# Constant rows of the score stacks: transfers from a row of ones in place of GpSimd memsets

## The reference

```python
x = x + L0_xattn(layernorm(x), ctx, ctx)          # linear attention to the context
x = x + L0_attn(layernorm(x), pos)                # attention over the batch axis
x = x + L0_ffn(layernorm(x))                      # 8 routed experts (top 2) and 2 shared
x = x + L1_xattn(layernorm(x), ctx, mask)         # softmax attention, 16 heads, 4096 keys
x = x + L1_attn(layernorm(x))                     # pre-norm self-attention with RoPE, and an MLP
x = x + L1_ffn(layernorm(x))                      # self-attention, then 8 experts (top 2)
...
scores = jnp.einsum('bhqd,bhkd->bhqk', q, k)
attn = jax.nn.softmax(scores, axis=-1)
out = jnp.einsum('bhqk,bhkd->bhqd', attn, v)
```

## Time and profile before

| | |
|---|---|
| median of 3 timed runs | 2186.85 us |
| the profiled execution, its own time | 2169.82 us |
| its span | 2168.1 us |
| TensorE (PE) busy | 1772.3 us, 82% |
| VectorE (DVE) busy | 1378.9 us, 64% |
| ScalarE (ACT) busy | 1063.2 us, 49% |
| GpSimd (POOL) busy | 464.2 us, 21% |
| granted TensorE clock, mean | 0.899 |

### The profile page before, as it was taken

One profiled execution on the slowest core, in us unless ns is written; L12 is line 12 of the kernel. 1 busy time (PEld: TensorE's weight loads), 2 busy tenths in 40 slices (PEclk: granted clock), 3 DMA queues, 4 the chain that ended last, 5 costly groups with the idle time before them and its releaser, 6 DMA issues.

```text
span 2168.1 us, 35268 instructions
## 1 busy us (share of the span) xinstructions
PE 1772.3 (82%) x14036; PEld 978.8 (45%) x14036; DVE 1378.9 (64%) x2137; ACT 1063.2 (49%) x1834; POOL 464.2 (21%) x347
## 2 busy tenths in 40 slices
PE   7998948888769888945999999999995578757876
PEld 5566635555547777621333333333332244523443
DVE  2231264251076999859999999999917654236456
ACT  3311112666543666410999999999980034112510
POOL 3212132676413666530000000000002000200000
PEclk9998969999978999975999999999997688968968
DMA  7113011777625565337335352433002611063100
GB/s 288 54 63 131 1 39 33 228 233 229 201 69 176 190 200 191 93 53 110 78 64 96 54 106 54 86 75 74 22 2 30 79 16 40 20 83 35 41 0 20
DMA packets 134880, 198.15 MB, mean 91 GB/s; under 512 B 20886, under 2 KB 100136, under 8 KB 130476
## 3 DMA queue, kind: packets, MB, share of 16 engines
q1 hardware_dynamic: 133052, 191.56, 35.2%
q0 software_dynamic: 1664, 4.33, 0.7%
HBM read 144.55 MB, written 50.99 MB: 90 GB/s over the span
## 4 chain that ended last, share of the span: by engine, by line
DVE 39%; PE 39%; SPq 7%; DMA 5%; issue 5%; POOL 3%; ACT 3%; DVEq 0%; ACTq 0%; POOLq 0%
DVE mx_part L2103 24%; SPq L754 4%; PE bank L1143 3%; PE pair L1484 3%; DVE w_lo L1924 3%; PE pair L1176 2%; DVE mx L2193 2%; PE bank L1279 2%; PE bank L999 2%; PE bank L248 2%; PE bank L1388 2%; PE bank L306 2%; DMA xT<-x_slots 1%; PE bank L1043 1%; PE pair L1338 1%
## 5 line engine op out<-in xcount | busy, mean ns | idle before, releaser
L1653 ACT ACTIVATE pexp_all<-bank 128x512 f32<-128x512 f32 x1024 | 551.9, 596 | 94.6 <-PE bank L1293 81.1
L2103 DVE TENSOR_REDUCE mx_part<-pair 128x2 f32<-128x1024 f32 x512 | 582.9, 1213 | 13.3 <-PE pair L1265 11.1
L1279 PE MATMUL bank<-pexp_all,vst 128*17 128x256 f32 x4096 | 321.6, 386 | 6.0 <-issue 6.0
L1265 PE MATMUL pair<-kst,qs 49*128 49x512 f16 x1024 | 210.1, 407 | 41.1 <-DVE mx_part L2103 28.3
L1293 PE MATMUL bank<-qs,kst 52*128 52x256 f16 x2048 | 203.4, 271 | 0.0
L1265 PEld LDWEIGHTS pair<-kst,qs 49*128 49x128 f16 x1024 | 50.4, 93 | 269.6 <-DVE mx_part L2103 215.3
L1293 PEld LDWEIGHTS bank<-qs,kst 52*128 52x128 f16 x2048 | 121.0, 95 | 56.8 <-ACT pexp_all L1653 18.4
L1663 ACT ACTIVATE pexp_all<-pair 128x1024 f32<-128x1024 f32 x64 | 65.5, 1023 | 151.9 <-PE pair L1408 150.3
L2453 POOL TENSOR_SCALAR neg_grp<-mx_grp 128x8 f32<-128x8 f32 x16 | 3.7, 233 | 602.6 <-DVE mx_grp L2123 602.6
L1279 PEld LDWEIGHTS bank<-pexp_all,vst 128*17 128x17 f32 x4096 | 68.8, 95 | 114.5 <-issue 104.9
L1176 PE MATMUL pair<-w_hi,hid_hi 128*128 128x256 f16 x368 | 101.0, 275 | 4.6 <-DVE w_lo L1924 4.6
(11 more groups left out here) (313 smaller groups left out, 3453.2 us busy)
## 6 DMA issues: line engine op xcount, KB each, us to landing
w_f<-in_w_all SPq DMA_DIRECT2D x34, 1024.0 KB, 6.7
kst<-k_scr SPq DMA_DIRECT2D x192, 128.0 KB
v_scr<-v_st SPq DMA_DIRECT2D x64, 272.0 KB, 2.6
vst<-v_scr SPq DMA_DIRECT2D x16, 1088.0 KB, 5.5
ctx_sb<-in_ctx SPq DMA_DIRECT2D x16, 1024.0 KB, 4.9
cT<-in_ctxT SPq DMA_DIRECT2D x32, 512.0 KB, 4.5
k_scr<-k_hi SPq DMA_DIRECT2D x128, 64.0 KB, 2.6
k_scr<-k_lo SPq DMA_DIRECT2D x128, 64.0 KB, 2.3
```

The costliest lines, as they stand in the source:

```text
L1265: last = pe.matmul(pair[n % 2][:, e * 512:(e + 1) * 512], qs[g % NBK][rws, p, qt * P:(qt + 1) * P], kst[g % NBK][rws, p, kb * 512:(kb + 1) ...
L1279: last = pe.matmul(bank[3][32 * h:32 * h + HV, 0:S], vst[g % 2][:, c, h * HV:(h + 1) * HV], unit_exp[n % NUE][:, p * S:(p + 1) * S], start ...
L1653: act.activation(unit_exp[n % NUE], bank[SCORE_BANKS[n % 3]], ACT.Exp, scale=SCALE).then_inc(s_exp, 1)
L2103: dve.tensor_reduce(mx_part[:, :, 2 * p + qt, kb], pair[n % 2][:, :].rearrange("p (e k) -> p e k", e=2), X_AXIS, ALU.max).then_inc(s_mx, 1)
```

## The change

The memsets of `kst`, `self_k` and `self_q` are taken out. A small tile `ones` is set once, at the start, and stored as one row of 8192 ones in memory (`ones_scr`). From there the rows of ones are loaded: rows 49 to 51 and 113 to 115 of each `kst` (`one_rows`, 3 rows of 16 KB to a load), counted on the semaphore of the group's queries, and rows 64 to 66 of `self_k` in two loads. `qs` is still filled by memsets, now in a row. `R_MAX` becomes 64; in the self-attention the first pass sums 64 rows and the second 67.

```diff
-R_MAX = 65
+R_MAX = 64
...
+        ones_scr = dram("ones_scr", [1, 2 * S2], F16)
+        ones = sb("ones", [P, 2 * S2 // P], F16)
...
-            sp.wait_ge(s_pool, 1)
+            sp.wait_ge(s_pool, 2)
+            sp.dma_start(ones_scr.rearrange("o (p n) -> (o p) n", p=P), ones[:, :]).then_inc(s_xz, 16)
...
-            sp.wait_ge(s_init4, 1)
+            def one_rows(i):
+                for e in range(2):
+                    at = HALF * e + X_MAX
+                    sp.dma_start(kst[i][at:at + 3, :, :],
+                                 ones_scr.rearrange("o (p n) -> o p n", p=2).to_broadcast([3, 2, S2])).then_inc(s_q[i], 16)
+
+            sp.wait_ge(s_x, 3 * T)
+            sp.wait_ge(s_xz, 32)
             load_keys(0, 0)
             load_keys(0, 1)
...
-            sp.wait_ge(s_init4, 2 * NBK)
+            sp.wait_ge(s_init4, NBK)
             load_queries(0)
+            one_rows(0)
             load_queries(1)
+            one_rows(1)
...
             load_queries(2)
+            one_rows(2)
+            one_rows(3)
...
             def self_io(sa, scr):
                 def max_rows(half):
-                    sa.wait(sp, "rows_set", 3)
...
+                for i in range(2):
+                    sp.dma_start(sa.k[R_MAX:R_MAX + 3, 32 * i:32 * i + 32, :],
+                                 ones_scr.rearrange("o (h n) -> o h n", n=S).to_broadcast([3, B * H // 2, S]))\
+                        .then_inc(signals["rows_set"].s, 16)
...
-                    pe.wait_ge(s_q[g % NBK], 96 * (g // NBK + 1))
+                    pe.wait_ge(s_q[g % NBK], 32 + 96 * (g // NBK + 1))
...
-                        sa.wait(pe, "rows_set", 3)
...
-                        last = pe.matmul(bank[n % 2][:, i * S:(i + 1) * S], sa.q[:, h, qt * P:(qt + 1) * P],
-                                         sa.k[:, h, :], start=True, stop=True)
+                        last = pe.matmul(bank[n % 2][:, i * S:(i + 1) * S], sa.q[0:R_MAX, h, qt * P:(qt + 1) * P],
+                                         sa.k[0:R_MAX, h, :], start=True, stop=True)
...
+                    if n == 0:
+                        sa.wait(pe, "rows_set", 33)
...
-                        last = pe.matmul(pair[n % 2][:, h * S:(h + 1) * S], sa.k[:, g * GH + h, c * P:(c + 1) * P],
-                                         sa.q[:, g * GH + h, :], start=True, stop=True)
+                        last = pe.matmul(pair[n % 2][:, h * S:(h + 1) * S], sa.k[0:R_MAX + 3, g * GH + h, c * P:(c + 1) * P],
+                                         sa.q[0:R_MAX + 3, g * GH + h, :], start=True, stop=True)
...
             steps.link(pool.memset(zeros[:, :], 0.0))
+            steps.link(pool.memset(ones[:, :], 1.0))
...
             for i in range(NBK):
-                pool.memset(wide(kst[i][:, :, :]), TWO_ONES).then_inc(s_init4, 1)
                 pool.memset(qs[i][:, :, :], UNMASK_ROW).then_inc(s_init4, 1)
...
                 pool.memset(sa.v[:, :, :, HD:HV], 1.0).then_inc(signals["rows_set"].s, 1)
-                sa.wait(pool, "rows_set", 1)
-                pool.memset(wide(sa.k[64:128, :, :]), TWO_ONES).then_inc(signals["rows_set"].s, 1)
-                sa.wait(pool, "rows_set", 2)
-                pool.memset(wide(sa.q[64:128, :, :]), 0.0).then_inc(signals["rows_set"].s, 1)
```

More of the change, by code:

```diff
@@ L48 @@
 SENTINEL = -5.0
-TWO_ONES = float(np.array([1.0, 1.0], dtype=np.float16).view(np.float32)[0])
 HV = HD + 1
@@ L560, in build @@
             "qk1_loaded": Counted("second_stacks_loaded", 16 * SELF_LOADS),
-            "rows_set": Counted("constant_rows_set", 3), "vproj": Counted("v_product", T),
+            "rows_set": Counted("constant_rows_set", 1 + 2 * 16), "vproj": Counted("v_product", T),
             "vtaken": Counted("v_copied", T), "s1": Counted("scores_first_pass", B * H),
@@ L2418, in _ @@
             pool.wait_ge(s_route, PLACED)
-            pool.wait_ge(s_xz, 16)
+            pool.wait_ge(s_xz, 32)
             for t in range(T):
@@ L2438, in _ @@
             pool.wait_ge(s_x, 3 * T)
-            def wide(ap):
-                return ap.rearrange("p h n -> p (h n)").bitcast(F32)
             for i in range(NBK):
-                pool.memset(wide(kst[i][:, :, :]), TWO_ONES).then_inc(s_init4, 1)
                 pool.memset(qs[i][:, :, :], UNMASK_ROW).then_inc(s_init4, 1)
```

## The result

The changed kernel is slower: 2202.14 us, median of 20 runs (2185.88 to 2224.76), against 2187.69 us for the kernel before in as many (2181.25 to 2194.95). The ratio is 1.0061 (95%: 1.0042 to 1.0081); two runs of the changed kernel count as slow, 2223.93 and 2224.76 us, and ratios are taken without such runs. The forecast was 2154.3 us, in a range from 2147 to 2166. The profiled execution took 2201.63 us (span 2199.9), at a mean granted clock of 0.876 where before it was 0.899.

A forecast was written before the change was run, and what follows sets the result against it. The prediction took the chain of waits as the bound, with GpSimd memsets holding up VectorE. Removing 35.0 us and adding 2.4 saved 32.6, so 2186.85 became 2154.3 us, range 2147 to 2166.

The forecast's parts named there:

- What bounds: Cross-attention and self-attention norms: the chain of waits bounds; GpSimd memsets hold up VectorE's TENSOR_SCALARs by a lock per instruction.
- what is removed: Delays of VectorE's norm steps: 11.8 us in the cross-attention, 11.6 in each self-attention layer, 35.0 us in all.
- What is added: Twelve loads of ones, a store and a small memset: 2.4 us before the cross-attention's first sum, otherwise nothing.
- the estimate of 2.6: Landing of the ones before the cross-attention's first sum: 2.6 us from three engines' bandwidth, making the sum 0.3 us better.
- The rival of the late ones: Cross-attention, group 0: a pair of loads of ones takes 10 us, giving 2164 us; chance 0.08.
- The second layer's weights: Second self-attention layer: weights needed 11.6 us sooner just fit before the projections; nothing, up to 1 us if not.
- 64 and 67 rows in place of 128 in the self-attention's sums: Both passes of the self-attention: a matmul's time goes by columns, so fewer rows change nothing, 0 us.
- The slower rival: Self-attention's second passes: the clock stays at half, up to 69 us more for both, 2223 us in full; chance 0.04.
- its own turning point of 47%: Self-attention's second passes: the saving becomes a loss once the clock is at half for over 47% of the stage.
- Its sign: Self-attention's second passes: a granted clock below 1.00 in the profile after would show the half-clock case.
- The drain rival: Self-attention's second pass: switching between 64 and 67 rows drains the array, 0.19 us each, 8.4 us, 2162.7; chance 0.10.
- the store and the small memset: First stage, far ahead of the first reader: storing the row of ones and setting its tile cost nothing.

The follow-up runs named there:

- 12: The kernel before, with GpSimd waiting for the end of VectorE's norm before its memsets in all three places; 2136.75 us, ratio 0.9875 to the kernel before.
- 13: The kernel before, unchanged, profiled again on a fourth chip; 2159.3 us in its one run, beside a median of 2162.29 us.
- 14: The changed kernel, unchanged, profiled and timed again on the fourth chip (the second series); 2172.09 us against 2162.29 for the kernel before, ratio 1.0038.
- 1 to 8: Follow-up kernels on two chips, varying rows of the self-attention's sums, loads of ones and memsets; ratios to the kernel before from 0.9894 to 1.018.
- 9 to 14: Later kernels on two further chips: zero rows, later memsets, combined versions, and both original kernels again; ratios of the edited ones to the kernel before 0.9806 to 0.9913.
- Kernel 1: The kernel before with only the self-attention's sums cut to 64 and 67 rows, all memsets kept; 2227.61 us, ratio 1.018 to the kernel before.
- the best version found: The changed kernel with 128-row sums, early ones, second-layer memsets behind the norm, mask conversion on VectorE; 2122.75 us, ratio 0.9806 to the kernel before.

## Why the prediction was wrong

**What bounds, and what is removed: right.** L212 and L232 have the durations that were taken, and L228 has 0.57 us for 0.45: it ends at 966.16, as the last of the four `qs` memsets does. The head of the cross-attention and the two self-attention norms gave 8.3, 11.8 and 13.7 us; 12 moves only the memsets, and every L211 and L227 of these places is at its usual length. The Trainium skill (SBUF — State Buffer, Who interferes with whom) describes this as a port pair of VectorE and GpSimd that one instruction holds exclusively to its end; the earlier trace rows (in between two memsets), the 0.57 us of L228 and the CAST of 12 agree.

**What is added: right in kind, 1.2 us short.** The landing took 4.1 us for 2.9 taken (4.0 to 5.5 over all profiles with late ones); the estimate of 2.6 beside it was lower still. The rival of the late ones, at 10 us a pair, did not happen. The second layer's weights did not hold it up: that stage gained 13.7.

**The step that failed** is the term "64 and 67 rows in place of 128 in the self-attention's sums ... Time goes by columns; nothing". Its row was right for what it shows: at one clock, 67 rows take what 128 take (1.06 us for four at half clock, before and after). It was taken from a stretch at full clock, and told nothing of which clock these sums would be given. Measured in place of 0: +33.2 us in the second passes of the first pair of profiles and +33.6 in those of 13 and 14; in the first passes +4.2 and +0.5, so the larger figure there does not repeat. That is 37.4 and 34.1 us, about the 35.3 that the rest gained. Of this the drain is about 2.4. The row hid it in a second way: it starts at 1760, and the stage begins at 1745.3, with 8 us at mostly half clock (0.94 over the whole stage).

**The slower rival was the right mechanism, with a chance of 0.04.** Its arithmetic comes near, in part by luck. It put 34.5 us a layer on a stage wholly at half clock, priced on 45 of its 60 us. The mean clock of 0.69 and 0.65 is 62% and 70% of the stage at half, against 12% before. That gives 0.50 x 34.5 + 0.58 x 34.5 = 37 us, near the 33.2 measured, and both shares lie above its own turning point of 47%. Its sign, a clock below 1.00 in the second passes, was badly set, though: the kernel before has 0.94 there. What I held against it was that the cross-attention, with 49 and 52 rows, has a clock of 1.00. That was a false parallel. There two heads lie at partitions 0 and 64 of one buffer, and their sums run at the same time: in the trace of the kernel before the sums of L1293 start in pairs, 3 to 4 ns apart and 0.11 us from pair to pair, at about 0.27 us each (around 1200 us). In the self-attention sum follows sum 0.11 us apart at full clock. Besides, the page after has 321.4 us of weighing sums of 128 rows (L1295) there beside 210.0 and 203.2 us of sums of 49 and 52. And the stretch has fewer pauses: TensorE is busy 97% of the time in it, and 88% in the piece of the stage at issue. Which of these keeps the clock up there was not tried.

**The drain rival** was real, but 0.11 us a place and not 0.19, and at 11 places a layer and not 22, as only the way into the 64 rows costs: 2.4 us and not 8.4. Why a place costs less than the lone pair that it was priced from was not tried.

**What stays open.** Stage by stage the two pairs of profiles give +0.2 us (above) and +1.8 us (13 and 14, from the last `x` update to the end) for the part with all the changed work, while the timed runs give 14 and 10 us. The rest lies ahead of it: 31.6 and 9.8 us. The traces split that at the first sum of the MoE block's shared expert (`x_s_hi`, L1143 before, L1159 after).

- From there to the last `x` update the stage has two lengths, and in the later profiles they go with the chip: 326 to 333 us in the eight profiles of 1 to 8, whose chips give the kernel before 2186.9 and 2186.5 us, and 300 to 308 us in the six of 9 to 14 (2164.9 and 2162.3 us). The changed kernel's profile has 329.9, and the first profile of the kernel before 305.3, although its timed runs have 2187.69. Kernel 1, with the instructions of the kernel before in this stage, has 328.0. So 24.6 of the 31.6 us are not the change's; the first profile of the kernel before is short there, as its 2169.82 us against a lowest timed run of 2181.25 also say.
- Up to there it is 626.8 and 633.8 us, and 624.9 and 637.3 in 13 and 14. All four profiles without the store and the small memset (before, 1, 12, 13) lie between 619.7 and 626.8, mean 624.3; the twelve with them between 625.3 and 637.3, mean 630.7. So these two, which the prediction put at nothing, may cost some 6 us. The groups overlap, and the store was not tried by itself.

Rows and store together would leave 7 to 8 us over the kernel before, within the interval of the second series (3 to 13 us) and a little under that of the first (9 to 18). Part of the rest may be that the point at which the clock rises moves from run to run: the runs of the changed kernel spread over 39 us, those of before over 14. Experiment 1 by its timed runs alone, 41 us (31 to 48), less the 35.3 saved, gives 6 us (-4 to 12) without any store.

## What to carry to other kernels

Cutting the rows of a matmul saves no time by itself, and it can take the fast clock away from a stage that has pauses; before padding is removed from sums, look at how far into its stage the granted clock rises (here 8 us), and after it, at that clock first. Rows of zeros kept the clock as well as rows of ones. A GpSimd memset costs what it holds up on VectorE: here where it started mattered more than how the rows were made, and two added waits got 28 of the 42 us that the best version found.

## What the runs showed of the hardware that was not expected

- The clock that was granted in this stage depended on the rows of the sums. With 64 and 67 rows TensorE was busy 36.4 of 40 us and stayed at 1.2 GHz; in 1, for 20 of 20 us. With 128 rows the same stage reached 2.4 GHz after about 8 us. The Trainium skill (TensorE: Matmul & The Clock Gate, What's actually happening) says that the clock follows how busy TensorE has been; these runs show that busy time alone does not tell it.
- Zeros in both operands count as rows: 60.2 and 59.2 us, clock 0.95 and 0.97.
- Entering sums of 64 rows from sums of 67 or 128 cost 0.11 us at 1.2 GHz and, from 128, 0.10 at 2.4 GHz; from 68 rows to 68, nothing.
- Two loads of 3 rows of 16 KB each, behind six query loads, took 4.1 us from the end of their issue to the sum that they released (4.0 to 5.5 in all such profiles), about as long as the 4.4 us of a load of maxima and longer than the 1.4 us after six query loads alone.
- Two sums of 52 rows at partitions 0 and 64 ran at the same time: starts 3 to 4 ns apart, 0.27 us each.
